# Expert routing: bias products on four row groups, the slot inversion in two column groups and three pieces, shares marked by GpSimd

## What is computed

```
logits = t @ gate_w.T + gate_b                 # t: 1088 x 192, 8 experts
top_val, top_idx = top_k(logits, 2)
score = softmax(top_val)
cw = zeros((T, 8)).at[arange(T), top_idx].add(score)
for e in range(8):
    he = gelu(t @ w1[e].T + b1[e])             # 192 -> 768
    ye = he @ w2[e].T + b2[e]                  # 768 -> 192
    out = out + cw[:, e:e+1] * ye
result = layernorm(h + x + out)
```

## Time and profile before

| | us |
|---|---|
| median of 3 runs | 833.82 |
| lowest and highest | 833.5, 836.08 |
| the profiled execution | 831.77 |
| its span in the trace | 830.0 |

### The profile page before, as it was taken

The page is one execution under the profiler, slowest core; times in us unless marked ns, Lnnn a source line. Parts: engine busy times, 40 slices in busy tenths (PEclk is TensorE's granted clock), DMA queues, the critical chain, the costliest instruction groups (busy, mean ns, idle before and its releaser), DMA issues. The chain is left out here.

```text
span 830.0 us, 17940 instructions
## 1 busy us (share of the span) xinstructions
PE 715.0 (86%) x6425; PEld 623.9 (75%) x6425; DVE 533.1 (64%) x1058; ACT 443.6 (53%) x864; POOL 427.9 (52%) x375
## 2 busy tenths in 40 slices
PE   4999999999999902579898889999899988999980
PEld 4888888888888802578788778776567767999980
DVE  3788888888888711356555555588759774555543
ACT  1778878778787831334444444343264231666640
POOL 3667666666666435377777777200300022567751
PEclk9999999999999956689999999999999975999995
DMA  9855448964788449555555555310000576233324
GB/s 233 220 150 153 132 139 232 242 184 133 194 236 231 197 95 210 191 157 164 152 143 152 147 149 152 101 38 2 1 1 2 230 216 187 44 58 57 55 29 125
DMA packets 78516, 114.85 MB, mean 138 GB/s; under 512 B 8791, under 2 KB 58108, under 8 KB 78076
## 3 DMA queue, kind: packets, MB, share of 16 engines
q1 hardware_dynamic: 61246, 76.80, 33.2%
q0 software_dynamic: 14336, 35.40, 16.6%
q10 hardware_dynamic: 2880, 1.90, 0.7%
HBM read 91.83 MB, written 22.25 MB: 137 GB/s over the span
## 5 line engine op out<-in xcount | busy, mean ns | idle before, releaser
L592 PE MATMUL psum<-power,tT 128*128 128x192 f32 x864 | 160.2, 341 | 65.8 <-DVE tT L719 65.2
L592 PEld LDWEIGHTS psum<-power,tT 128*128 128x128 f32 x864 | 145.8, 197 | 77.5 <-issue 41.7
L533 POOL DMA_INDIRECT rows<-power_table,rank_row x144 | 145.5, 1010 | 66.1 <-issue 54.3
L327 PE MATMUL ps<-dft,fold 112*112 112x97 f32 x1536 | 168.0, 264 | 10.9 <-POOL fold L294 10.9
L327 PEld LDWEIGHTS ps<-dft,fold 112*112 112x112 f32 x1536 | 167.3, 180 | 11.4 <-issue 10.8
L719 DVE SCALAR_TENSOR_TENSOR tT<-rows,swaps,scaled 128x384 f32<-128x384 f32 x144 | 82.7, 616 | 119.1 <-ACT scaled L647 118.8
L647 ACT ACTIVATE scaled<-rows,swaps 128x384 f32<-128x384 f32 x144 | 80.6, 607 | 138.1 <-DMA rows<-power_table,rank_row 138.1
L301 POOL TENSOR_TENSOR ss<-uv 97x388 f32<-97x388 f32 x96 | 82.2, 877 | 97.1 <-ACT uv L367 97.1
L399 DVE TENSOR_TENSOR folded<-ps,far 112x388 f32<-112x388 f32 x192 | 98.4, 553 | 46.7 <-ACT far L355 46.5
L294 POOL TENSOR_TENSOR fold<-img 112x896 f32<-112x896 f32 x48 | 103.4, 2154 | 14.8 <-DMA img<-in_x 8.7
L416 DVE TENSOR_TENSOR uv<-ps,odd 97x388 f32<-97x388 f32 x192 | 97.7, 549 | 2.6 <-ACT odd L360 2.6
(11 more groups left out here) (174 smaller groups left out, 933.9 us busy)
## 6 DMA issues: line engine op xcount, KB each, us to landing
img<-in_x SPq DMA_DIRECT2D x48, 784.0 KB, 5.2
power_table<-power SPq DMA_DIRECT2D x16, 576.0 KB
power<-in_w_tok SPq DMA_DIRECT2D x3, 1728.0 KB, 10.2
power<-in_w SPq DMA_DIRECT2D x8, 579.0 KB, 7.6
power<-in_w SPq DMA_DIRECT2D x4, 1152.0 KB, 10.8
rows<-power_table,rank_row POOLq DMA_INDIRECT x144, 3.1
power_table<-power SPq DMA_DIRECT2D x1, 1200.0 KB
power_table<-power SPq DMA_DIRECT2D x1, 1072.0 KB, 15.1
```

The source lines that it names most:

```text
L327: last = pe.matmul(ps1[0:HALF, j % 2, i, col:col + FREQ], fold[:, j // UPG % FOLD_RING, part, x0:x0 + HALF], dft[:, part * FREQ:(part + 1) ...
L533: pool.indirect_dma_start(out=rows[:, j % RING, half, :], out_offset=None, in_=table[0:RECORDS if j % CHUNKS < PLAIN else RECORDS + P * (L ...
L592: last = pe.matmul(ps[:, q % 2, 0:DIM], points[:, j % SWAPPED, c, s].rearrange("p h b -> p (h b)"), wt[:, c, s, chunk, :], start=(chunk == ...
```

## The change

`cw` gets 32 columns for each tile (8 used, the others zeroed by a memset ahead of the last `top_two`), so that three transposes of 128 x 128 put four tiles' shares on the lanes 0 to 7, 32 to 39, 64 to 71 and 96 to 103. One ScalarE copy replaces three. The nine bias products take their 8 rows from these four groups of 32 lanes, and `b2` is repeated on the same lanes; each group writes to a bank of its own. Only the last of them signals.

The slot products are split in two halves of 64 output lanes (36 products, 72 records), and wait for their marks in three pieces of six. VectorE now makes `sent`'s token half first, then `at_lane` in three pieces. The share half is made by GpSimd, in two operations at the head of its queue. VectorE adds the bias of the first three tiles before it waits for `found`, and that of the six others after `target`.

```diff
@@ -1275,8 +1275,11 @@
     pick = sb("pick", [P, TOPK, TT, EXPERTS])
-    cw = sb("cw", [P, TT, EXPERTS])
-    cwT = sb("cwT", [EXPERTS, TPAD])
+    ROW_GROUPS = 4
+    GROUP = P // ROW_GROUPS
+    SETS = -(-TT // ROW_GROUPS)
+    cw = sb("cw", [P, SETS * ROW_GROUPS, GROUP])
+    cwT = sb("cwT", [P, SETS, P])
     both = sb("both", [P, TT + 1, EXPERTS])
@@ -1295,6 +1298,8 @@
     sent = sb("sent", [P, TOPK * TT, 2, MT])
+    tiles_at = at_tile.rearrange("p (k t) m -> p k t m", k=TOPK)
+    sent_of = sent.rearrange("p (k t) a m -> p k t a m", k=TOPK)
     unused = sb("unused", [P, MT])
@@ -1315,13 +1320,22 @@
     cw_set, cw_tr, cwT_done, b2_mm, biased = S("cw_set"), S("cw_tr"), S("cwT"), S("b2_mm"), S("biased")
+    shares_marked = S("shares_marked")
     stat, powed, final, out_done = S("stat"), S("pow"), S("final"), S("out")
...
     w2_now = W["q_all"]
-    BIAS_BANK = (6, 7, 0, 5, 4)
+    BIAS_BANK = (6, 7, 0, 5)
+    PIECES = 3
+    PIECE = TOPK * TT // PIECES
+
+    def bias_at(t):
+
+        bank = BIAS_BANK[t % ROW_GROUPS] if t // ROW_GROUPS < 2 else 4
+        at = t // ROW_GROUPS % 2 * DIM
+        return psum[:, bank, at:at + DIM]
     U = 4
@@ -1381,6 +1395,12 @@
     def program_pool(pool):
+        pool.wait_ge(share_set, 1)
+        pool.wait_ge(ah, 4)
+        for k in range(TOPK):
+            last = pool.tensor_tensor(sent_of[:, k, :, 1, :], tiles_at[:, k],
+                                      share[:, :, k, None].to_broadcast([P, TT, MT]), ALU.mult)
+        last.then_inc(shares_marked, 1)
         pool.wait_ge(W["rows_stored"], STORED)
@@ -1421,19 +1441,25 @@
 
-        pe.wait_ge(cw_set, 1)
+        pe.wait_ge(cw_set, 2)
+        for n in range(SETS):
+            last = pe.transpose(psum[:, 3, n * P:(n + 1) * P],
+                                cw[:, n * ROW_GROUPS:(n + 1) * ROW_GROUPS, :].rearrange("p t e -> p (t e)"), W["identity"])
+        last.then_inc(cw_tr, 1)
+        pe.wait_ge(cwT_done, 1)
         for t in range(TT):
-            last = pe.transpose(psum[0:EXPERTS, 3 + t // 4, t % 4 * P:(t % 4 + 1) * P], cw[:, t, :], W["identity"])
-        last.then_inc(cw_tr, 1)
-        pe.wait_ge(cwT_done, 3)
-        for t in range(TT):
-            pe.matmul(psum[:, BIAS_BANK[t // 2], t % 2 * DIM:(t % 2 + 1) * DIM], cwT[:, t * P:(t + 1) * P], W["b2"],
-                      start=True, stop=True).then_inc(b2_mm, 1)
-
-        pe.wait_ge(marked, 3)
-        for n in range(TOPK * TT):
-            last = pe.matmul(psum[:, 2, 0:2 * MT], at_lane[:, n, :], sent[:, n].rearrange("p a m -> p (a m)"),
-                             start=(n == 0), stop=(n == TOPK * TT - 1))
+            rows = slice(t % ROW_GROUPS * GROUP, t % ROW_GROUPS * GROUP + EXPERTS)
+            last = pe.matmul(bias_at(t), cwT[rows, t // ROW_GROUPS, :], W["b2"][rows, :], start=True, stop=True)
+        last.then_inc(b2_mm, 1)
+
+        for piece in range(PIECES):
+            pe.wait_ge(marked, 2 + piece)
+            if piece == 0:
+                pe.wait_ge(shares_marked, 1)
+            for n in range(piece * PIECE, (piece + 1) * PIECE):
+                for half in ROW_HALVES:
+                    last = pe.matmul(psum[half, 2, 0:2 * MT], at_lane[:, n, half], sent[:, n].rearrange("p a m -> p (a m)"),
+                                     start=(n == 0), stop=(n == TOPK * TT - 1))
         last.then_inc(found, 1)
@@ -1484,9 +1510,7 @@
         act.wait_ge(cw_tr, 1)
-        for b in range(3):
-            n = min(4, TT - 4 * b) * P
-            act.activation(cwT[:, b * 4 * P:b * 4 * P + n], psum[0:EXPERTS, 3 + b, 0:n], ACT.Copy).then_inc(cwT_done, 1)
+        act.activation(cwT[:, :, :].rearrange("p n t -> p (n t)"), psum[:, 3, 0:SETS * P], ACT.Copy).then_inc(cwT_done, 1)
 
@@ -1531,6 +1555,8 @@
         for n in range(NC):
+            if n == NC - 1:
+                dve.memset(cw[:, :, :], 0.0).then_inc(cw_set, 1)
             top_two(n)
@@ -1571,7 +1597,8 @@
         dve.wait_ge(share_set, 1 + TOPK)
-        dve.tensor_tensor(cw[:, :, :], shared[:, 0], shared[:, 1], ALU.add).then_inc(cw_set, 1)
+        dve.wait_ge(cw_set, 1)
+        dve.tensor_tensor(cw[:, 0:TT, 0:EXPERTS], shared[:, 0], shared[:, 1], ALU.add).then_inc(cw_set, 1)
 
@@ -1616,26 +1643,23 @@
                           at_f[:, 1, :, None].to_broadcast([P, N, MT]), ALU.is_equal).then_inc(ah, 1)
-        dve.tensor_tensor(at_lane[:, :, :], W["lanes"][:, None, :].to_broadcast([P, N, P]),
-                          at_f[:, 0, :, None].to_broadcast([P, N, P]), ALU.is_equal).then_inc(marked, 1)
         dve.wait_ge(ah, 4)
-        dve.wait_ge(share_set, 1)
-        tiles_at = at_tile.rearrange("p (k t) m -> p k t m", k=TOPK)
-        sent_of = sent.rearrange("p (k t) a m -> p k t a m", k=TOPK)
         for k in range(TOPK):
...
         last.then_inc(marked, 1)
-        for k in range(TOPK):
-            last = dve.tensor_tensor(sent_of[:, k, :, 1, :], tiles_at[:, k],
-                                     share[:, :, k, None].to_broadcast([P, TT, MT]), ALU.mult)
-        last.then_inc(marked, 1)
+        for piece in range(PIECES):
+            part = slice(piece * PIECE, (piece + 1) * PIECE)
+            dve.tensor_tensor(at_lane[:, part, :], W["lanes"][:, None, :].to_broadcast([P, PIECE, P]),
+                              at_f[:, 0, part, None].to_broadcast([P, PIECE, P]), ALU.is_equal).then_inc(marked, 1)
         dve.tensor_copy(tile_expert[:, :], tile_f[:, :]).then_inc(slot_done, 1)
         c.end()
-        for t in range(TT):
-            dve.wait_ge(b2_mm, min(TT, t // 2 * 2 + 2))
-            dve.tensor_tensor(x_all[:, t, :], psum[:, BIAS_BANK[t // 2], t % 2 * DIM:(t % 2 + 1) * DIM], x_all[:, t, :],
-                              ALU.add).then_inc(biased, 1)
+        def add_bias(t):
+            dve.tensor_tensor(x_all[:, t, :], bias_at(t), x_all[:, t, :], ALU.add).then_inc(biased, 1)
+
+        dve.wait_ge(b2_mm, 1)
+        for t in range(NC):
+            add_bias(t)
         dve.wait_ge(found, 1)
@@ -1643,6 +1667,8 @@
+        for t in range(NC, TT):
+            add_bias(t)
@@ -1743,7 +1769,7 @@
-        moe = dict(gate_b=constant("gate_b", [P, EXPERTS], broadcast=True), b2=constant("b2", [EXPERTS, DIM]),
+        moe = dict(gate_b=constant("gate_b", [P, EXPERTS], broadcast=True), b2=constant("b2", [P, DIM]),
@@ -1874,7 +1900,7 @@
         w1=np.concatenate([w1_rows.transpose(0, 4, 2, 1, 3, 5).reshape(EXPERTS, P, THIRDS * W1_HALF), i["L0_ffn_b1"].reshape(EXPERTS, HT, P).transpose(0, 2, 1)], 2).transpose(1, 0, 2),
-        w2=i["L0_ffn_w2"].transpose(0, 2, 1).reshape(EXPERTS * HT, P, DIM), b2=i["L0_ffn_b2"])
+        w2=i["L0_ffn_w2"].transpose(0, 2, 1).reshape(EXPERTS * HT, P, DIM), b2=np.repeat(np.pad(i["L0_ffn_b2"], ((0, P // 4 - EXPERTS), (0, 0)))[None], 4, 0).reshape(P, DIM))
     nc = _bacc.Bacc("TRN2", target_bir_lowering=False, num_devices=1)
```

## The result

Over all runs taken side by side (17 of each kernel) the changed kernel has a median of 830.57 us against 834.59 us, and the ratio is 0.9943 with a 95% interval from 0.9924 to 0.9963: 3.1 to 6.3 us faster, 4.8 in the middle (the two medians lie 4.0 us apart). The forecast was 5.0 us.

What follows compares the result with a forecast made beforehand. TensorE's work ahead of the expert loop was taken as the bound, VectorE's marks next. The inversion ending 5.3 us earlier, less 0.3 for the fetch, gave -5.0 us: 828.8 us median, range 825.3 to 832.6.

Steps and rivals of the forecast that it cites:

- What bounds it: Ahead of the expert loop: TensorE's work is the path, VectorE's marks next; a shorter bias loop alone gives 0.7 us.
- Transposes, copy, bias products: Before the inversion: three transposes 0.65 us, one copy for three, bias products 1.5 to 6.1 us, covered by VectorE's marks.
- The dear end: Bias products on four row groups: no overlap at all, 6.1 us, over at 688.1, costing about nothing.
- Marks and GpSimd's pair: Ahead of the inversion: GpSimd's pair blocks VectorE for 1.1 us, so piece one is marked at 687.75.
- The inversion: Slot products in two column groups: each pays its own weight load, 3.8 us plus 0.4 tail, 4.2 us in all.
- rival E: Slot products: both column groups' loads run in series with the columns, 13.5 us, kernel slower at 838.5 us; chance 0.06.
- The fetch: First fetch of rows after the inversion: later x_all stores run beside it, charged 0.3 us, bounds 0 and 1.95.
- a sign of being wrong: First fetch landing much later than 3 us after its start, named as something that would show the prediction wrong.
- The clock: First hidden layer: low-clock stretch costing 1.7 us is kept; it could vanish (-1.7) or come twice (+1.7).
- B: Marks and clock: GpSimd blocks nothing or the clock rises early, -6.1 to -7.8 us, 826.9 in the middle; chance 0.17.
- C: Marks: GpSimd is kept out until VectorE's series is over, -3.2 us, 830.6; chance 0.14.
- D: After the inversion: fetch waits 1.95 us for stores, low clock costs 1.7 more, -1.7 us in all, 832.1; chance 0.15.

Runs made afterwards that it cites:

- bias_part_alone: Kernel before with only the change's bias part (three transposes, one copy, row groups), marks in the old order; ratio 0.9973 (0.9936 to 1.0009).
- old_bias_part: Changed kernel with the bias part as before: nine transposes, three copies, nine bias products one behind another; ratio 0.9959 (0.993 to 0.9989) of the kernel before.
- gpsimd_twice: Changed kernel with a second pair of the same products on GpSimd, into an unread tile; whole kernel not timed, VectorE's three pieces 3.76 us.
- additions_first: Changed kernel with all nine bias additions ahead of the wait for the last slot product; ratio 0.992 (0.9891 to 0.995) of the kernel before.
- late_stores: Changed kernel with share pair on VectorE, two busy-work rounds before the slot products, second-sums zeroing and x_all stores after the third fetch; ratio 0.9897 of the kernel before.
- busy_to_the_loop: late_stores with four busy-work rounds behind the last slot product for two, one more behind the first rows' transposes; median 821.66 us, ratio 0.9876 of the kernel before.
- pe_kept_busy: Changed kernel with two rounds of busy work on TensorE between bias products and slot products; ratio 0.9939 (0.9916 to 0.9961) of the kernel before.
- busy_once_ahead: busy_to_the_loop with one round of busy work ahead of the slot products in place of two; ratio 0.9927 (0.9894 to 0.996) of the kernel before.

## Why the prediction was right

- **What bounds it.** Right. With the bias products gone, VectorE's marks end the wait (L1653 in the chain after). That a shorter bias loop alone is worth little was right in kind: 0.7 us foreseen, 0.1 measured by bias_part_alone. The memset was hidden, as said.
- **Transposes, copy, bias products.** 0.55 and 0.49 us against 0.65 and some 0.5. The four row groups overlap: 18 records in 1.24 us at the high clock and 2.28 at the low one, where 1.5 was said for full overlap. The claim that the edit's speed is covered by the marks held for four groups, at either clock. The dear end, none overlapping, was put at 7.3 us after T0; against the measured start at 6.81 it would have cost 0.5 us and not nothing. With the old transposes and copies too the bias products end at 8.5, and that costs 1.6 us (old_bias_part).
- **Marks and GpSimd's pair.** Piece one was forecast at 687.75 - 680.80 = 6.95 us after T0, and the inversion started at 6.81. The step behind it was right, the engines exclude each other and GpSimd gets its turn between two VectorE operations (gpsimd_twice). One size in it was off: I had the pair hold VectorE up for 1.1 us, and it did so for 0.72, 0.36 for each product. So the move cost 0.13 us against the pair on VectorE, where I had 0.5. A part of the difference was lost again ahead of the marks, where at_tile starts 3.85 us after T0 against 3.72 before.
- **The inversion.** 4.2 us forecast, 4.11 measured, and 7.92 without column groups at the same clock. That each column group pays only for its own load, side by side with the other, is borne out: 72 records, 53 ns apart with the tail taken off ((4.08 - 0.31)/71, a record lasting 307 ns). The rival E, loads in series with the columns, is out.
- **The fetch.** 3.58 us in place of 2.96: 0.6 us lost where I charged 0.3. The mechanism was right (additions_first 3.16, late_stores 2.85), the term was too small by half. The landing at 3.58 us also comes near what I had named as a sign of being wrong.
- **The clock.** I kept the loss in the first layer as it was. It grew: 3.95 + 2.42 for 3.69 + 2.06, 0.6 us, and the second tile's transposes also ran slowly. This is the term that the sum had at nothing, inside its stated bounds. From T0 to H3 the profile shows 4.0 us: 5.5 from the earlier end of the inversion (5.3 forecast), less 0.6 for the fetch, 0.6 for the layers and 0.3 for what lies between. The runs show 4.8, with 4.0 inside their interval. So the steps up to found are borne out, what follows it was put too low, 1.5 us in place of 0.3, and that the runs come as near to 5.0 as 4.8 is in part luck. The lower end of the range, 825.3, doesn't follow from my terms: B with the clock's gain (-7.8) and the denser inversion at the high clock (-1) are 825.0.
- **The rivals.** Of B only a part came true, and in other kernels: the profile of the changed kernel had the low clock in its inversion. C is out: GpSimd's pair ended at 689.57, within the first piece. D came true in small, 1.5 of its 3.65 us. What I did not see is how large that side is: a fixed loss of 1.7 us was treated as a given, when busy_to_the_loop shows that it and more can be had back. What makes the clock fall ahead of the first layer stays open.

## What to carry to other kernels

Ask of each shortened step which wait is late next, and price the edits together: the same row-group edit was worth 0.1 us alone and 1.6 us with the marks made earlier. A step limited by loading weights, with few columns to move, is worth splitting into column groups. And where TensorE waits a few microseconds ahead of dense work, look at the granted clock behind the wait, and hold back transfers that nobody needs yet from the moment when a small, urgent one is issued.

## What the runs showed of the hardware

- Two column groups of 64 lanes load weights side by side: 72 records of 64 columns in 4.08 us against 36 of 128 columns in 7.92, both at the low clock. Four row groups of 8 rows ran 18 records of 192 columns in 2.28 us at the low clock, against 6.12 in series at the same clock, and in 1.24 at the high one.
- A GpSimd product of 128 x 216 and VectorE's operations on two SBUF tensors took turns, with both queues full. The GpSimd product ended 0.41 us after the VectorE operation that ran when it started, whether its recorded time was 0.69 us (behind a short one) or 1.27 (behind a long one), and the next VectorE operation was 0.36 us longer. A recorded duration on an engine thus contains its wait for the other.
- Behind 3.5 us of busy work, most of it at the low clock, the clock was 1.00 (pe_kept_busy); behind 2.1 us of it and 0.9 us of idling it was 0.50 (busy_once_ahead), as it had been throughout; and behind 6.12 us of bias products in series without a gap it was 0.50 too (old_bias_part).
- The 680 us ahead of T0 differed by up to 7 us between profiles of nearly equal programs. What makes them differ was not looked into.
